# A fused transformer chain: the causal mask of the maxima copied into PSUM by VectorE, and all score units cut to 512 columns

## What is computed

```python
q, k, v = split(x @ w_qkv)                 # q: 32 heads, k and v: 8 heads, 16 columns each
q, k = rope(q), rope(k)
scores = einsum('bhsd,bhtd->bhst', q, repeat(k, 4)) * scale
scores = where(causal, scores, -inf)       # key t is seen by query s if t <= s
probs = softmax(scores, axis=-1)
out = einsum('bhst,bhtd->bhsd', probs, repeat(v, 4))
x = layernorm(x + out @ w_o)
```

## Time and profile before

| what | value |
|---|---|
| runs shown | 2558.08, 2558.59, 2547.9 us |
| profiled execution | 2559.52 us |
| its span on the core | 2557.8 us |
| mean granted TensorE clock | 0.966 |
| TensorE, VectorE, ScalarE, GpSimd busy | 2414.6, 1401.4, 1027.9, 502.9 us |
| weight loads of TensorE | 1275.9 us |

### The profile page before, as it was taken

The page is one execution under the profiler, slowest core; times in us unless marked ns, Lnnn a source line. Parts: engine busy times, 40 slices in busy tenths (PEclk is TensorE's granted clock), DMA queues, the critical chain, the costliest instruction groups (busy, mean ns, idle before and its releaser), DMA issues.

```text
span 2557.8 us, 35349 instructions
## 1 busy us (share of the span) xinstructions
PE 2414.6 (94%) x12760; PEld 1275.9 (50%) x12760; DVE 1401.4 (55%) x3211; ACT 1027.9 (40%) x1983; POOL 502.9 (20%) x634
## 2 busy tenths in 40 slices
PE   7887798999999999999999999999987999999998
PEld 6664354545455454555555555555543444444443
DVE  6755787757657566676777767677741111111111
ACT  5663356444445354454545445465541100011000
POOL 4521222222312112131312222222220000000000
PEclk8788799999999999999999999999998999999999
DMA  5000323211202012130312023122121000010000
GB/s 169 1 1 1 116 83 109 70 48 55 95 24 94 18 39 98 53 102 26 119 33 93 29 85 108 54 81 93 45 94 65 0 17 0 0 49 0 16 0 16
DMA packets 90177, 140.81 MB, mean 55 GB/s; under 512 B 8464, under 2 KB 63760, under 8 KB 89232
## 3 DMA queue, kind: packets, MB, share of 16 engines
q1 hardware_dynamic: 90016, 138.71, 16.4%
HBM read 81.93 MB, written 52.56 MB: 53 GB/s over the span
## 4 chain that ended last, share of the span: by engine, by line
PE 63%; issue 26%; DVE 6%; ACT 3%; DMA 1%; POOL 1%; SPq 0%; POOLq 0%; DVEq 0%; ACTq 0%
PE ps L1377 10%; PE ps L1337 9%; PE ps L1319 8%; PE ps L1297 7%; PE ps L1356 7%; PE ps L1216 5%; PE ps L1392 4%; PE ps L1294 3%; PE ps L1424 2%; PE ps L1401 2%; DVE negmax L2065 2%; PE ps L1250 1%; PE ps L1244 1%; ACT big L1632 1%; DVE x L2114 1%
## 5 line engine op out<-in xcount | busy, mean ns | idle before, releaser
L1632 ACT ACTIVATE big<-ps 128x512 f32<-128x512 f32 (+1 forms) x1056 | 571.2, 560 | 644.3 <-PE ps L1319 622.6
L2065 DVE TENSOR_REDUCE negmax<-ps 128x1 f32<-128x512 f32 (+3 forms) x1056 | 648.0, 637 | 304.2 <-PE ps L1297 299.7
L1814 POOL TENSOR_SCALAR_AFFINE_SELECT big<-big 128x512 f32<-128x512 f32 x384 | 256.2, 670 | 1100.8 <-ACT big L1632 1100.3
L1195 PE MATMUL ps<-xt,big 128*128 128x512 f32 x896 | 391.8, 600 | 3.4 <-ACT xt L1500 3.4
L1319 PE MATMUL ps<-big 99*128 99x512 bf16 (+3 forms) x1536 | 372.7, 303 | 12.7 <-DVE rest L2190 6.8
L1297 PE MATMUL ps<-big 96*128 96x128 bf16 (+3 forms) x1536 | 382.4, 303 | 0.0
L1377 PE MATMUL ps<-big,xt 128*128 128x512 f32 (+1 forms) x768 | 296.2, 492 | 0.7 <-ACT xt L1653 0.7
L1195 PEld LDWEIGHTS ps<-xt,big 128*128 128x128 f32 x896 | 172.3, 193 | 220.9 <-issue 220.9
L1294 PE MATMUL ps<-cbf 128*128 128x128 bf16 (+2 forms) x1056 | 260.4, 247 | 11.5 <-DMA big<-scr_q 5.4
L1337 PE MATMUL ps<-big,vs 128*32 128x512 f32 (+3 forms) x3072 | 248.0, 441 | 2.3 <-POOL big L1814 2.2
L1297 PEld LDWEIGHTS ps<-big 96*128 96x128 bf16 x1536 | 143.5, 98 | 205.7 <-issue 166.7
(11 more groups left out here) (214 smaller groups left out, 2574.6 us busy)
## 6 DMA issues: line engine op xcount, KB each, us to landing
big<-scr_q SPq DMA_DIRECT2D x96, 384.0 KB, 3.9
scr_q<-big SPq DMA_DIRECT2D x48, 384.0 KB, 2.5
scr_q<-big SPq DMA_DIRECT2D x48, 256.0 KB, 2.9
big<-scr_k SPq DMA_DIRECT2D x48, 192.0 KB, 3.4
big<-in_ffn_gu SPq DMA_DIRECT2D x14, 512.0 KB, 7.8
scr_q<-big SPq DMA_DIRECT2D x48, 128.0 KB, 2.7
big<-in_attn_w SPq DMA_DIRECT2D x3, 1536.0 KB, 6.7
scr_k<-big SPq DMA_DIRECT2D x12, 384.0 KB, 2.5
```

Source lines behind the costliest of these rows:

```text
L1195: mm = pe.matmul(ps[:, 2 * (m % 2) + k, :], w(c, m), xt[:, c, :], start=(c == 0), stop=(c == DC - 1))
L1632: act.activation(probs_of(i), bank_of("exp", g, i)[:, 0:len(heads) * w], ACT.Exp, scale=1.0 / 16 if attn_of(n) == 1 else 0.25).then_inc(ma ...
L1814: pool.affine_select(block_, block_, [[0, GQ], [1, P]], ALU.is_ge, zero, base=0, channel_multiplier=-1).then_inc(made["cut"], 1)
L2065: dve.tensor_reduce(negmax[:, p % 2, q, h0:h0 + n], bank_of("max", p, u)[:, 0:n * w].rearrange("p (h k) -> p h k", h=n), AX.X, ALU.max, ne ...
```

## The change

The mask of the maxima is no longer written by TensorE. The units are cut anew, ten a group, all of 512 columns (`MAX_UNITS`):

- four X units, one a head: query blocks 2 and 3 of the head against key blocks 0 and 1 (two matmuls of 256 columns);
- four D units, one a query block: the diagonal block of each of the four heads (four matmuls of 128 columns). VectorE first copies the mask four times over the bank (`mask_first`, a copy of 512 elements a partition from bf16 to f32), and TensorE adds to it (`start=False`). Such a bank is taken only where its last holder wrote all 512 columns (`whole`);
- two Y units: block 1 against key block 0, and block 3 against key block 2 (four matmuls of 128 columns each).

The maxima of the blocks go into `peaks`, and `split_max` first reduces them over the blocks (128 elements to 32), once a pair. The exponentials have ten units of 512 columns: key block 3's 128 columns stand behind block 1's 384. The weighting takes key block 0 as half 0 and blocks 1, 3, 2 as half 1; both are due after the group's last exponential (`LAG` 2). It has no banks of its own now: all eight are shared, with at most 4 for maxima, 4 for exponentials and 5 for the rest.

```diff
-UNITS = 11
+UNITS = 10
 LEAD = 12
-LAG = 3
-BANKS, MOST = (0, 1, 2, 3, 4, 5), (3, 3, 3, 6)
+LAG = 2
+BANKS, MOST = (0, 1, 2, 3, 4, 5, 6, 7), (4, 4, 5, 8)
...
+MAX_UNITS = ("X", "D", "X", "D", "X", "D", "X", "D", "Y", "Y")
+KEY_ENDS = (3, 7, 9, 7)
...
+def exp_unit(i):
+    if i < 4:
+        return [(0, i, 0)]
+    if i < 8:
+        return [(1, i - 4, 0), (3, i - 4, 3 * P)]
+    return [(2, 2 * (i - 8), 0), (2, 2 * (i - 8) + 1, 2 * P)]
...
+    if name == "preset":
+        return [("max_full", (n, k[1] - 2) if k[1] >= 2 else (n - 1, k[1] + 2 * UNITS - 2))] if n or k[1] >= 2 else [("begin", ())]
...
-            for half, last in ((0, 7), (1, UNITS - 1)):
+            for half, last in ((0, UNITS - 1), (1, UNITS - 1)):
...
             def max_scores(p, u):
...
-                pe.matmul(bank[:, :, w - P:w], identb, mask_q.unsqueeze(1).broadcast_to((P, n, P)),
-                          start=True, stop=False, skip_group_check=True)
-                for k, h in enumerate(heads):
-                    mm = pe.matmul(bank[:, k, :], qt[0:KROWS, g % 6, h, q * P:(q + 1) * P], kt[0:KROWS, p % 3, g % 2, 0:w],
-                                   start=False, stop=True, skip_group_check=True)
+                if kind == "D":
+                    wait_made(pe, "preset", p, u)
+                    for h in range(GQ):
+                        mm = pe.matmul(bank_of("max", p, u)[:, h * P:(h + 1) * P], of(h, at), against(at, at + 1),
+                                       start=False, stop=True, skip_group_check=True)
+                elif kind == "X":
+                    bank = bank_for("max", p, u)
+                    for k in range(2):
+                        mm = pe.matmul(bank[:, 2 * P * k:2 * P * (k + 1)], of(at, 2 + k), against(0, 2),
+                                       start=(k == 0), stop=True, skip_group_check=True)
...
             def weigh(g, half_):
-                wait_made(pe, "cut", g, 2 * half_ + 1)
+                wait_made(pe, "cut", g, 2 * half_)
...
-                for key in (2 * half_, 2 * half_ + 1):
+                for key in (1, 3, 2) if half_ else (0,):
...
             def weights_of(g, i):
-                    wait_made(act, "pv_full", g - 1, key // 2)
+                    wait_made(act, "pv_full", g - 1, int(i > 3))
...
+            def mask_first(p, u):
+                if p == 0:
+                    dve.wait_ge(constants, 17)
+                name, key = flow.released(flow.bank_before["max", (p, u)])
+                wait_made(dve, name, *key)
+                dve.tensor_copy(bank_of("max", p, u).rearrange("p (h k) -> p h k", h=GQ), mask_q.unsqueeze(1).broadcast_to((P, GQ, P))
+                     ).then_inc(made["preset"], 1)
...
             def split_max(p):
...
+                then(dve.tensor_reduce(negmax[:].rearrange("p q h -> p h q"),
+                                       peaks[:, p % 2].rearrange("p g h q s -> p (g h) q s"), AX.X, ALU.min))
```

More of the change, by code:

```diff
@@ L128, in side_work @@
     if before >= 0:
-        dealt.append((49.5, ("lnx", "d", before)))
+        dealt.append((4.5 * UNITS, ("lnx", "d", before)))
         if attn_of(before) == 1:
@@ L221, in pieces @@
     if kind == "max":
-        q, heads, w = max_unit(k[1] % UNITS)
-        n = len(heads)
-        last = [("DVE", "split", k[:1], 900)] if k[1] == 2 * UNITS - 1 else []
-        return [("PE", "max", k, columns(n * (P + w), 0.43)), ("DVE", "negmax", k, 190 + columns(n * w, 1.05))] + last
+        last = [("DVE", "split", k[:1], 1100)] if k[1] == 2 * UNITS - 1 else []
+        return MASKS[max_unit(k[1])[0] == "D"](k) + [("DVE", "negmax", k, 190 + columns(512, 1.05))] + last
     if kind == "shift":
@@ L574, in try_out @@
         free = dict.fromkeys(todo, 0)
-        held = {H_BANKS[q]: ("th", ("h", (NL, q, 0))) for q in (2, 3)}
+        held = {H_BANKS[q]: ("th", ("h", (NL, q, 0))) for q in range(NB)}
         known = {}
@@ L598, in try_out @@
                     bank = None
-                    if engine == "PE" and name not in NO_BANK and self.unit(name, key) not in self.bank:
+                    if (name == "preset" or engine == "PE" and name not in NO_BANK) and self.unit(name, key) not in self.bank:
                         bank, begin = self.room(held, ended, name, begin)
@@ L618, in try_out @@
                     self.bank_before[unit] = held[bank][1]
-                held[bank] = (name, unit)
+                held[bank] = (unit[0], unit)
             free[engine] = begin + ns
@@ L626, in room @@
     def room(self, held, ended, name, begin):
-        group = lambda of: 0 if of in ("max", "shift") else 1 if of == "exp" else 3 if of in FRONT else 2
+        group = lambda of: 0 if of in ("max", "preset", "shift") else 1 if of == "exp" else 3 if of in FRONT else 2
         mine = [b for b in held if group(held[b][0]) == group(name)]
@@ L632, in room @@
             when = 0
+            if name == "preset" and (b not in held or not self.whole(held[b][1])):
+                continue
             if b in held:
@@ L685, in unit, with whole @@
         return name, k
+    @staticmethod
+    def whole(unit):
+        kind, k = unit
+        return kind in ("max", "exp", "gate", "up", "down", "dense", "base") or kind == "proj" and k[2] == 0
     @staticmethod
@@ L1284, in max_scores @@
                 g = 2 * p + u // UNITS
-                q, heads, w = max_unit(u % UNITS)
+                kind, at = max_unit(u)
                 if u == 0:
@@ L1316, in exp_scores @@
                         pe.wait_ge(ready, 1)
-                bank = bank_for("exp", g, i)[:, 0:n * w].rearrange("p (h t) -> p h t", h=n)
-                for k, h in enumerate(heads):
-                    mm = pe.matmul(bank[:, k, :], kt[0:SROWS, p % 3, g % 2, key * P:(key + 1) * P],
-                                   qt[0:SROWS, g % 6, h, key * P:S], start=(k == 0), stop=True, skip_group_check=True)
+                bank = bank_for("exp", g, i)
+                for key, h, at in exp_unit(i):
+                    mm = pe.matmul(bank[:, at:at + S - key * P], kt[0:SROWS, p % 3, g % 2, key * P:(key + 1) * P],
+                                   qt[0:SROWS, g % 6, h, key * P:S], start=(at == 0), stop=True, skip_group_check=True)
                 mm.then_inc(made["exp_full"], 1)
@@ L2304, in flow_vectors @@
                         half_bias()
+                    elif kind == "preset":
+                        mask_first(*k)
                     elif kind == "negmax":
```

98 lines of the change are left out of this document (50 added, 48 removed).

## The result

| kernel | median | runs | span | granted clock |
|---|---|---|---|---|
| before | 2558.34 us | 2547.9 to 2558.86 (4) | 2557.8 us | 0.966 |
| changed | 2629.77 us | 2624.88 to 2637.21 (4) | 2623.1 us | 0.942 |

The ratio is 1.0292, 95% interval 1.0252 to 1.0331: 2.9% slower. The forecast was 2501 us, in a range of 2470 to 2545.

What follows compares the result with a forecast made beforehand. TensorE was taken to bound the stages changed, as long as VectorE keeps up. Stage gains of 27 + 26 + 5 + 5 less 4.5 us at the opening gave 58.5, so 2559.5 - 58.5 = 2501 us, range 2470 to 2545.

Steps and rivals of the forecast that it cites:

- The waits that come: TensorE's D units wait for VectorE's copies, with a microsecond or two of cover; ScalarE's slack hides the later weighting.
- The stage sums: Gains kept per stage under VectorE's load: 27, 26, 5 and 5 us, less 4.5 at the opening, 58.5 us in all.
- TensorE's gain, 84.5 us: Mask matmuls leave TensorE: 0.88 us a group, 96 groups, the most the change can give by columns.
- The copy's price: VectorE's 384 mask copies take 0.60 us each (0.33 to 0.71); net 230 us more VectorE work over the run.
- Recut at nothing: Scores cut into 32 matmuls a group instead of 16, same 5120 columns, charged no TensorE time.
- The opening: VectorE's first chain before the first exponential grows from 12.1 to 16.8 us; 4.5 us lost.
- The slower one: Rival: TensorE waits at its queue's head for the mask, 0.30 us a copy, 115 us in all; 2590 us, 7%.
- VectorE as the bound: Rival: VectorE bounds both loaded stages, where no gain is kept; 26 us gained, 2533 us, 17%.
- whole gain: Rival: VectorE is never late and TensorE keeps all 84.5 us; 2475 us, 13%.
- short matmuls: Rival: TensorE's 128-column matmuls cost more than their columns, 0.08 us each, 29 us in all; 2530 us, 5%.
- late weighting: Rival: ScalarE's queue stops at each group for the weighting, costing TensorE 58 us; 2559 us, 8%.
- signs of error: Loaded-stage TensorE below 94% with VectorE above 95%; copies under 0.45 us; granted clock falling (500 to 1800); long ScalarE weighting waits.

Runs made afterwards that it cites:

- e7: e1 with the weighting as before the change: two banks of its own, LAG 3, first half due after the eighth exponential; 2566.23 us.
- e1: The changed kernel without VectorE's copies: TensorE writes each D unit's mask with one matmul of 512 columns; 2514.57 us.
- e4: The changed kernel with no mask in the maxima at all: no copy and no mask matmul; 2454.14 us.
- e12: e4, order unchanged, plus an unread VectorE reduce of the mask behind each X unit's reduce; 2499.32 us.
- e14: The changed kernel's order and banks, with an unread VectorE reduce in place of each copy and no TensorE wait for it; 2601.18 us.
- e15: e14, but TensorE waits before each D unit for the VectorE reduce that stands in the copy's place; 2624.49 us.
- e18: The changed kernel, its planner reckoning a copy at 100 ns instead of 700 and allowing it six units ahead instead of two; 2506.01 us.
- e3: The changed kernel with copies allowed up to six units of maxima ahead of their unit instead of two; 2554.90 us.
- e6: The changed kernel with the 384 mask copies moved from VectorE to ScalarE, planned anew; 2501.61 us.
- e11: e6 with the ScalarE copies allowed six units ahead of their D unit instead of two; 2474.50 us.
- e2: The changed kernel, order kept, each copy writing only 8 of 128 columns of its four blocks; 2586.78 us.
- e9: e1, order unchanged, plus an unread VectorE reduce of the mask behind each X unit's reduce; 2560.35 us.
- e5: e1, planned anew, with each D unit waiting for VectorE's reduce of the unit before, no work added; 2564.84 us.

## Why the prediction was wrong

The way from before to the change, each step the difference of two medians. The prices are those of this way; in another order of steps they can differ, as the tie's 50 and 40 us do.

| step | runs | us |
|---|---|---|
| all units 512 columns | before to e7 | +8 |
| weighting in the common banks, in one piece | e7 to e1 | -52 |
| the mask matmuls that are left in e1 go | e1 to e4 | -60 |
| VectorE's 384 x 512 elements, order kept | e4 to e12 | +45 |
| the change's order and banks | e12 to e14 | +102 |
| TensorE waits for that place in VectorE's queue | e14 to e15 | +23 |
| the copy in place of the reduce, with its wait for a bank | e15 to change | +5, within the noise |

**The step that failed** is in "The waits that come": "The order puts the copy right behind a unit's reduce, with an exponential and side work before the next D unit, so there is a microsecond or two of cover." It took one place of the order for the whole. In VectorE's queue 360 of the 384 copies follow the reduce of the unit just before their D unit (23 stand one unit earlier, and the first has no reduce ahead of it), and the planner, which reckons with the copy's wait, put the exponentials together. The order shown ahead of the prediction has a row of three matmuls of line 1355 in one piece. The stage sums then charged VectorE's load alone; 125 us of order and wait (102 + 23) had no term. In the profile of the change they show as two waits of TensorE, 68.3 us for the copies, which the prediction took to be covered, and 38.7 for the shift, of which it has no word on TensorE's side.

- **TensorE's gain, 84.5 us.** The matmuls went. Without any mask but with the columns' recut, it is 60 us for 384 matmuls that come to the same 84.5 by the price taken (e1 to e4): 24 us of it did not come through.
- **The copy's price** held: 0.60 us a slot. By the Trainium skill (VectorE: DVE Perf Modes, What auto-detection actually checks) it gets none of the faster modes, with 32 bits and PSUM on one side; at 683 ns against 683 of the reduce of as many elements the trace agrees. The term taken from it, 26 us lost to VectorE's load and the opening (84.5 - 58.5), was too small: the load alone costs 45 us with e4's order kept, e12, and 46 on e1.
- **Recut at nothing**: 8 us. TensorE's short matmuls are as forecast, 0.23 us for four.
- **The weighting and the banks** had no term of gain; they gave 52 us. This is why e12, with the whole load and a good order, came to 2499.3 us, close to the 2501 forecast: 52 us of gain not counted, and 51 of cost (8 of the recut, 24 of the matmuls, 19 of the load), cancel. That e12, and e18 with 2506, come so near to the forecast is luck and does not bear it out.
- **The opening**: the first matmul of the exponentials' scores is at 312.94 us for 298.11, +14.8 for a forecast of 4.5. By the copy of group 0's weighting (320.55 to 326.25 us), 5.7 are left. From the first to the last of the exponentials' scores it is 1649 us for 1599 before, 49 more, where some 60 less were forecast from the first score to the last.
- **The rivals.** The slower one (7%, 2590 us) had the sign, and its wait is there: 68.3 us on TensorE's matmuls before D units. But its price is not its own: the wait costs 23 us (e14 to e15), and the order and banks planned around it 102. VectorE as the bound (2533) didn't come, since in the order as it was VectorE never got past 84% in a stage. A whole gain, short matmuls and a late weighting are refuted by e12, e7 and e1.

Of the signs that I had named as signs of error, two came. The granted clock fell between 500 and 1800 us, to 0.96 in the second stage. And ScalarE waits for the weighting, 96.1 us from 500 to 1800 for 11.7 before, but in e1, which is 44 us faster than before, it waits 125.0 there, so this wait is not what costs. TensorE fell to 93% in the second stage, as named, but with VectorE at 83%, not above 95%: full load was not the reason.

## What to carry to other kernels

Where a planner or scheduler makes the order, a change of what an operation needs is a change of the order, and it has to be read as a whole: count, over the run, how long the pieces are in which each consumer gets its work, and how far ahead of its reader each new item stands in its queue, before any wait is priced. When a new wait shows up in a profile, read what else the bound engine waits for, and test the wait by an order kept and a wait removed (e14): here the 68 us for copies were worth 23, and when such a wait was taken away the one for the shift grew from 41.1 to 65.6 us. That second wait, 38.7 us in the change, stood in its profile from the start. And an operation that only fills a buffer may be given freedom in the plan (e3, e18) or to another engine (e6, e11) before it is called too dear: e18, e6 and e11 (2506, 2502, 2475 us) beat both kernels with the mask in place. e4, whose maxima run over masked keys too, is fastest at 2454.1; what is subtracted then is at least the true maximum, and whether that will do depends on how far masked scores may lie above the others.

## What was not expected of the hardware

- ScalarE copies 512 bf16 elements from SBUF to f32 in PSUM in 603 ns, VectorE in 683 ns.
- A copy of 4 x 8 elements (e2) still takes 184 ns on VectorE:

```profile
L2095 DVE CAST ps<-cbf 128x32 f32<-128x32 bf16 x384 | 70.5, 184 | 14.1 <-ACT big L1664 14.0
```

- Work for which nobody waits, added to VectorE with the order unchanged, cost 46 us (e9) and 45 us (e12), on two kernels 60 us apart. VectorE was 56 and 57% busy, and its busy time grew by 212 and 206 us: over a fifth of it comes through.
- The mean granted clock was lower where TensorE was idle more, but only roughly. By run: 0.970 in e1 (95% busy), 0.962 in e12 (94%), 0.950 in e14 (91%), 0.942 in the change (90%), but 0.968 in e5 (93%) and 0.954 in e3 (92%).
- TensorE's busy time isn't work alone. e9 has the matmuls, the order and nearly the clock of e1 (0.969 for 0.970), and 22.9 us more of it (2401.9 for 2379.0).
